# A decoder layer: an early expert tile from the first two batches, with its gate and up products and its transposes ahead of the index products

## Time and profile before

| | |
|---|---|
| median of three runs | 472.5 us (472.37 to 473.3) |
| the profiled execution | 473.93 us, of which 472.2 us are the span from its first to its last instruction |
| TensorE clock granted over the span | 0.955 of full |
| busy: PE, DVE, POOL, ACT | 420.8, 312.3, 221.1, 211.2 us |
| chain that ended last, by engine | PE 66%, DVE 17%, POOL 6%, issue 5%, DMA 3%, ACT 2% |
| batch 3 of the loop, to its last sum | about 250 to 309 us of the span |
| after the loop, to the first product of slot 1 | 309 to 345 us |
| slots 1 to 10 | 345 to 472 us, PE busy all through until 464 |

### The profile page before, as it was taken

The page is one execution under the profiler, slowest core; times in us unless marked ns, Lnnn a source line. Parts: engine busy times, 40 slices in busy tenths (PEclk is TensorE's granted clock), DMA queues, the critical chain, the costliest instruction groups (busy, mean ns, idle before and its releaser), DMA issues.

```text
span 472.2 us, 7846 instructions
## 1 busy us (share of the span) xinstructions
PE 420.8 (89%) x2560; PEld 212.2 (45%) x2561; DVE 312.3 (66%) x626; ACT 211.2 (45%) x412; POOL 221.1 (47%) x246
## 2 busy tenths in 40 slices
PE   4989588878998998989989899986999999999993
PEld 3444222333443443444434444354556666666652
DVE  3497778999987878878888786588214333334344
ACT  2456717564664557745577457612121111112220
POOL 2000615877986679967799578600551111111001
PEclk9998765798999999999999999999999999999997
DMA  9689940937365182756324430079120000000000
GB/s 237 91 279 108 301 144 12 146 119 115 89 138 110 68 134 70 134 180 199 137 78 169 159 112 0 1 287 361 55 55 11 12 4 9 11 11 11 11 1 9
DMA packets 39366, 49.36 MB, mean 105 GB/s; under 512 B 4664, under 2 KB 32673, under 8 KB 39334
## 3 DMA queue, kind: packets, MB, share of 16 engines
q1 hardware_dynamic: 36322, 46.65, 39.0%
q0 software_dynamic: 1056, 2.10, 1.5%
q10 hardware_dynamic: 1956, 0.21, 0.4%
HBM read 40.72 MB, written 8.91 MB: 105 GB/s over the span
## 4 chain that ended last, share of the span: by engine, by line
PE 66%; DVE 17%; POOL 6%; issue 5%; DMA 3%; ACT 2%; POOLq 0%; SPq 0%; DVEq 0%; ACTq 0%
PE ps L1181 16%; PE ps L1197 8%; PE ps L883 8%; PE ps L910 6%; PE ps L914 5%; PE ps L956 4%; PE ps L783 4%; DVE arena L1572 3%; DVE arena L1523 3%; DVE arena L1505 3%; PE ps L943 3%; PE ps L1189 2%; DMA arena<-arena 2%; POOL arena L655 2%; POOL arena L661 2%
## 5 line engine op out<-in xcount | busy, mean ns | idle before, releaser
L1372 ACT ACTIVATE arena<-ps 128x512 f32<-128x512 f32 x128 | 76.1, 595 | 84.9 <-PE ps L943 84.7
L1523 DVE TENSOR_REDUCE arena<-ps 128x2 f32<-128x512 f32 x128 | 86.6, 681 | 26.8 <-PE ps L914 22.7
L661 POOL TENSOR_TENSOR arena<-arena 128x512 f32<-128x512 f32 x60 | 76.8, 1279 | 36.2 <-DVE arena L1572 36.2
L655 POOL TENSOR_TENSOR arena<-arena 128x512 f32<-128x512 f32 x64 | 84.4, 1321 | 9.0 <-issue 8.8
L1181 PE MATMUL ps<-arena 128*128 x176 | 77.5, 593 | 0.7 <-ACT arena L1413 0.7
L1572 DVE TENSOR_TENSOR_SCAN arena<-ps,arena 128x512 f32<-128x512 f32 x60 | 72.8, 1214 | 0.5 <-DVE mv L1617 0.2
L883 PE MATMUL ps<-arena,identf 128*128 128x512 f32 x128 | 68.9, 625 | 0.0
L910 PE MATMUL ps<-arena 48*128 48x256 bf16 x256 | 52.7, 288 | 13.4 <-DVE arena L1523 10.0
L1331 ACT ACTIVATE ps<-arena 128x255 f32<-128x255 f32 x128 | 60.4, 473 | 1.9 <-DVEq L1726 1.9
L1839 DVE TENSOR_TENSOR arena<-arena,ps 128x1024 f32<-128x1024 f32 x11 | 13.4, 1222 | 59.9 <-ACT arena L1417 59.9
L731 POOL DMA_INDIRECT out<-rows_s,arena x11 | 10.8, 984 | 88.7 <-DVE rows_s L1868 80.5
(11 more groups left out here) (231 smaller groups left out, 524.7 us busy)
## 6 DMA issues: line engine op xcount, KB each, us to landing
arena<-bc_d SPq DMA_DIRECT2D x32, 512.0 KB, 4.4
arena<-in_L_ffn_Wg SPq DMA_DIRECT2D x8, 512.0 KB, 6.1
arena<-in_L_ffn_Wu SPq DMA_DIRECT2D x8, 512.0 KB, 5.9
arena<-in_L_ffn_Wd SPq DMA_DIRECT2D x4, 1024.0 KB, 11.7
arena<-kp_d SPq DMA_DIRECT2D x8, 384.0 KB, 7.9
arena<-qp_d SPq DMA_DIRECT2D x8, 384.0 KB, 10.8
qp_d<-arena SPq DMA_DIRECT2D x4, 384.0 KB, 8.5
kp_d<-arena SPq DMA_DIRECT2D x4, 384.0 KB, 8.4
```

The lines of the kernel that those rows point to most:

```text
L655: g.tensor_tensor(dBu[m % 3], dtu[:, :, b * SEQ:(b + 1) * SEQ], over_k(bcr[c % BC_RING][:, m % 2, 0, :]), ALU.mult).then_inc(dbu_ready, 1)
L661: g.tensor_tensor(h, h, over_k(bcr[m // 2 % BC_RING][:, m % 2, 1, :]), ALU.mult).then_inc(hc_ready, 1)
L1372: A(prob[2 * (slot % 2) + kt][:, pr * HALF:(pr + 1) * HALF], ps[:, 2 + n % 2, :], ACT.Exp).then_inc(p_ready, 1)
L1523: v.tensor_reduce(negm[b % 2][:, qt, 2 * pair:2 * pair + 2], ps[:, bank, :].rearrange("p (h k) -> p h k", h=2), axis=AX.X, op=ALU.max).the ...
```

## The change

**What is computed stays the same.** Slot 0 becomes an "early tile". Its 128 rows are the first 128 tokens of one expert among the first four token tiles (batches 0 and 1, 512 tokens in four experts, so at least one expert has 128). They are known once the logits of batch 1 are, in batch 3 of the loop. The remaining tokens fill slots 1 to 10 as before; there are still 11 slots.

- DVE gets five new groups inside batch 3: `early_experts` at (3, 2, 1), `early_counts` at (3, 3, 0), `early_choice` at (3, 4, 0), `early_ranks` at (3, 5, 0), `early_marks` at (3, 6, 0): 10, 3, 7, 7 and 4 instructions. PE gets `count_early` (two products, one more turn of the banks) at (3, 3, 0).
- POOL's `routing_constants` move from m = 56 to m = 49 and grow from ten fills to fourteen.
- PE picks the early rows (`pick_rows(EARLY, ...)`, 8 products) right after the loop, and ACT copies them (`take_x(0)`) ahead of its copy for the late logits.
- The gate and up product of slot 0 is cut into four halves. One stands ahead of `route_late(3)`, two ahead of the counting products, one behind them, in the places of 2, 10 and 10 of the fillers. Ahead of the first half PE waits for all gate and up weights and loads the expert's number.
- The picked rows of the old kind (8 tiles) now serve slot 1. `make_h(0)` on DVE stands behind the row masks, ahead of the index marks, and `turn_h(0)` on PE ahead of the index products. Slot 1 enters the loop without `gate_up(0)`, `turn_x(1)`, 8 fillers and `turn_h(0)` between the index products and it.
- POOL gathers slots 2, 0, 1 first; the first row handed to PE is slot 2.

On PE, behind the second transpose of the last batch (L1135; L1194 in the changed kernel) and up to the slots, there stood: fillers L871, the late logits L1111, the two counting products L1146 and L1147, the row picks L1154, the index products L1161.

The diff, cut to what matters:

```diff
@@ POOL: routing_constants, and where it is called
                 link(g.memset(resets, 1.0))
                 link(g.memset(resets[:, :, 0:1], 0.0))
+                link(g.memset(resets1, 1.0))
+                link(g.memset(resets1[:, :, 0:1], 0.0))
+                link(g.memset(placed[:, EXPERTS, :], 0.0))
+                link(g.memset(reached1[:, 0:1], 0.0))
...
-                if m == 3 * STATES + 8:
+                if m == 3 * STATES + 1:
                     routing_constants()
@@ PE: the loop, and after it
+            def count_early():
+                pe.wait_ge(early_oh, 1)
+                pe.wait_ge(consts, 4)
+                bank = turn()
...
+                        if b == BATCH - 1 and (qd, i) == (3, 0):
+                            count_early()
...
+            pe.wait_ge(y_out, BATCH)
+            pick_rows(EARLY, early_rows, early_ready)
             pe.wait_ge(x2_ready, 2 * (BATCH - 1))
             turn_late(BATCH - 2)
...
-            keep_warm(2, 5)
+            pe.wait_ge(wgu_in, 16 * 16)
+            pe.wait_ge(xcur_ready, 2)
+            first_expert = pe.value_load(estar_int[0:1, 0:1], min_val=0, max_val=EXPERTS - 1)
+            gate_up_half(0, first_expert)
             route_late(BATCH - 1)
-            keep_warm(10, 7)
+            for half in (1, 2):
+                gate_up_half(half, first_expert)
             pe.wait_ge(oh_ready, 1)
...
-            keep_warm(14, 4)
+            gate_up_half(3, first_expert).then_inc(gu_done, 1)
+            keep_warm(4, 4)
...
+            pick_rows(TT, first_rows, first_ready)
+            turn_h(0)
             pe.wait_ge(expert_ready, 1)
...
-            pe.wait_ge(wgu_in, 16 * 16)
-            gate_up(0, first_expert)
-            turn_x(1)
-            keep_warm(8, 6)
-            turn_h(0)
             pe.wait_ge(wd_in, 16 * 4)
             with pe.Fori(1, SLOTS - 1) as s:
@@ DVE: the new groups (each link() waits for its own instruction)
+            def first_of_max(tiles):
+                link(v.tensor_copy(run[:, tiles], oh[:, tiles, 0]))
+                v.tensor_copy(ohb[:, 0, tiles], oh[:, tiles, 0]).then_inc(logit_dve, 1)
+                for e in range(1, EXPERTS):
+                    link(v.tensor_tensor(ohb[:, e, tiles], oh[:, tiles, e], run[:, tiles], ALU.is_gt))
+                    link(v.tensor_tensor(run[:, tiles], run[:, tiles], oh[:, tiles, e], ALU.max))
+            def early_experts():
+                two = slice(0, EARLY)
+                link(v.tensor_reduce(lmax[:, two], lg[:, two, :], axis=AX.X, op=ALU.max))
+                link(v.tensor_tensor(oh[:, two, :], lg[:, two, :], lmax[:, two]..., ALU.is_ge))
+                first_of_max(two)
+                dve.sem_inc(early_oh, 1)
+            def early_counts():
+                bank = turn()
...
+                link(v.tensor_tensor_scan(out=incl1..., data0=resets1..., data1=ps[:, bank, n:2 * n], ...))
+                link(v.tensor_tensor(within1, incl1, earlier1, ALU.add))
+                link(v.tensor_tensor(within1, within1, total1, ALU.subtract))
+                dve.sem_inc(taken, 1)
+            def early_choice():
+                link(v.tensor_scalar(enough, incl1[:, :, EARLY - 1], float(P), None, ALU.is_ge))
+                link(v.tensor_tensor_scan(out=best, data0=ones32[:, 0:EXPERTS], data1=enough, ...))
...
+            def early_marks():
+                for t in range(EARLY):
+                    v.tensor_scalar(early_rows[t], lanes, float(P + 1), lane1[:, t:t + 1], ALU.add,
+                                    ALU.is_equal).then_inc(early_ready, 1)
...
+                        if b == BATCH - 1 and (qd, i) == (2, 1):
+                            dve.wait_ge(taken, turns.count)
+                            early_experts()
+                        if b == BATCH - 1 and (qd, i) == (3, 0):
+                            early_counts()
+                        if b == BATCH - 1 and (qd, i) == (4, 0):
+                            early_choice()
+                        if b == BATCH - 1 and (qd, i) == (5, 0):
+                            early_ranks()
+                        if b == BATCH - 1 and (qd, i) == (6, 0):
+                            early_marks()
@@ DVE: after the row masks of the slots
+            make_h(0)
...
+            link(v.tensor_tensor(e_of[:, 0:1], e_of[:, 0:1], estar, ALU.add))
```

More of the change, by code:

```diff
@@ L216, in decoder_layer @@
         run = carve(TT)
-        within = carve(EXPERTS * TT, EXPERTS, TT)
+        placed = carve((EXPERTS + 1) * TT, EXPERTS + 1, TT)
+        within, of_early = placed[:, 0:EXPERTS, :], placed[:, EXPERTS, 0:EARLY]
+        incl1 = carve(EXPERTS * EARLY, EXPERTS, EARLY)
+        within1 = carve(EXPERTS * EARLY, EXPERTS, EARLY)
+        resets1 = carve(EXPERTS * EARLY, EXPERTS, EARLY)
+        enough = carve(EXPERTS)
+        reached1 = carve(EXPERTS + 1)
+        best = carve(EXPERTS)
+        estar = carve(1)
+        estar_int = carve(1, dt=I32)
+        rank1 = carve(EARLY)
+        lane1 = carve(EARLY)
+        keep = carve(EARLY)
+        early_rows = [carve(P) for _ in range(EARLY)]
         incl = carve(EXPERTS * TT, EXPERTS, TT)
@@ L737, in _ @@
             pool.wait_ge(idx_ready, 1)
-            for s in (1, 0, 2):
+            for s in (2, 0, 1):
                 gather(s)
-            hand_row(1)
+            hand_row(2)
             for s in range(3, SLOTS):
@@ L1096, in expert_of, with gate_up_half, pick_rows, turn_h @@
                 return pe.value_load(e_int[0:1, bass.ds(s, 1)], min_val=0, max_val=EXPERTS - 1)
+            def gate_up_half(half, e):
+                w, fh = (wg_s, wu_s)[half // 2], half % 2
+                for k in range(KT):
+                    last = mm(ps[:, half, :], xcur[:, k, :], w[:, bass.ds((e * KT + k) * DFF + fh * HALF, HALF)],
+                              start=(k == 0), stop=(k == KT - 1))
+                return last
+            def pick_rows(tiles, marks, ready):
+                for t in range(tiles):
+                    pe.wait_ge(ready, t + 1)
+                    for k in range(KT):
+                        last = mm(ps[:, 7, k * P:(k + 1) * P], xres[:, t, k * P:(k + 1) * P], marks[t],
+                                  start=(t == 0 and k == 0), stop=(t == tiles - 1), skip_group_check=True)
+                last.then_inc(xt_pe, 1)
+            def turn_h(s):
+                pe.wait_ge(h_ready, s + 1)
+                for f in range(FT):
+                    last = nc.tensor.transpose(ps[:, 4 + f // 4, (f % 4) * P:(f % 4 + 1) * P],
+                                               hcur[:, f * P:(f + 1) * P], identf[:, :])
+                last.then_inc(ht_pe, 1)
             def turn_late(b):
@@ L1177, in gate_up @@
                 pe.wait_ge(xcur_ready, s + 2)
-                for w, b0 in ((wg_s, 0), (wu_s, 2)):
-                    for fh in range(2):
-                        for k in range(KT):
-                            last = mm(ps[:, b0 + fh, :], xcur[:, k, :],
-                                      w[:, bass.ds((e * KT + k) * DFF + fh * HALF, HALF)], start=(k == 0),
-                                      stop=(k == KT - 1))
-                last.then_inc(gu_done, 1)
-            def turn_h(s):
-                pe.wait_ge(h_ready, s + 1)
-                for f in range(FT):
-                    last = nc.tensor.transpose(ps[:, 4 + f // 4, (f % 4) * P:(f % 4 + 1) * P],
-                                               hcur[:, f * P:(f + 1) * P], identf[:, :])
-                last.then_inc(ht_pe, 1)
+                for half in range(4):
+                    last = gate_up_half(half, e)
+                last.then_inc(gu_done, 1)
             def down(s, e):
@@ new lines, in early_ranks @@
+            def early_ranks():
+                of_best = best.rearrange("p (e o) -> p e o", o=1).broadcast_to([P, EXPERTS, EARLY])
+                link(v.scalar_tensor_tensor(out=within1, in0=within1, scalar=1.0, in1=of_best, op0=ALU.add, op1=ALU.mult))
+                link(v.tensor_tensor(within1, within1, ohb[:, :, 0:EARLY], ALU.mult))
+                link(v.tensor_reduce(rank1, within1.rearrange("p e t -> p t e"), axis=AX.X, op=ALU.add))
+                link(v.scalar_tensor_tensor(out=lane1, in0=rank1, scalar=float(P), in1=rank1, op0=ALU.is_le, op1=ALU.mult))
+                link(v.tensor_scalar(of_early, lane1, -1.0, 0.0, ALU.add, ALU.max))
+                link(v.tensor_scalar(keep, lane1, 1.0, None, ALU.is_lt))
+                link(v.tensor_tensor(ohb[:, :, 0:EARLY], ohb[:, :, 0:EARLY],
+                                     keep.rearrange("p (o t) -> p o t", o=1).broadcast_to([P, EXPERTS, EARLY]), ALU.mult))
@@ L1777, in _ @@
             link(v.tensor_tensor(lg, lg, lmax3, ALU.subtract))
-            link(v.tensor_copy(run, oh[:, :, 0]))
-            v.tensor_copy(ohb[:, 0, :], oh[:, :, 0]).then_inc(logit_dve, 1)
-            for e in range(1, EXPERTS):
-                link(v.tensor_tensor(ohb[:, e, :], oh[:, :, e], run, ALU.is_gt))
```

(3 more changed lines are left out.)

70 lines of the change are left out of this document (43 added, 27 removed).

## The result

The changed kernel takes 477.24 us (median of 4 runs, 476.58 to 477.92), the kernel before 472.75 us in the same comparison: a ratio of 1.0094, 95% interval 1.0074 to 1.0114. It is slower by about 4.5 us. The forecast was 471.4 us and the range ended at 474.4 us.

The account below looks back on a forecast made before the run. PE bounds the slots, and batch 3, where PE, DVE and POOL have little room, and the tail count in full: 8.15 us cost less 9.2 us saved gives -1.05 us, so 472.5 becomes 471.4 us; range 466.8 to 474.4 us.

Parts of the forecast that it names:

- the second rival: Batch 3: TensorE's clock falls behind new waits; one fall costs 1.7 us (473.1 us), two give 474.8 us; chance 0.16.
- waits of 2.85 and 3.3 us: Batch 3: PE stands still behind `early_experts` (2.85 us) and `early_choice` (3.3 us), whose DVE instructions wait for POOL's.
- batch 3's waits: Batch 3: the new DVE groups and POOL's moved constants delay the loop by 0.1 + 2.85 + 1.4 + 3.3 + 0.5 = 8.15 us.
- the tail: Between loop and slots: slot 1's product starts at 335.9 instead of 345.07 us, 9.2 us saved (8.3 to 9.6).
- Rival 1: Batch 3: small DVE instructions slip between POOL's, so the groups cost 3.7 us; 467.0 us, chance 0.22.
- the three waits that it gave `early_choice`: Batch 3: three of its seven instructions wait for one POOL product each, until 283.4 us; the next copy moves 3.3 us.
- slot 1's product follows after some 0.15 us: Tail, on PE: gap between the index products' end at 335.76 us and slot 1's gate and up product.
- the register load: Tail, ahead of slot 0's first half: loading the expert's number on PE was taken as 0.3 us, between 0 and 1.
- 0.25 was booked: Tail: what is left of the early picks' push on the late logits, 0.25 us (0.1 to 0.4).
- Rival 3: Tail: returns only 8.3 us if the register load takes 1 us and late logits and counts hold DVE; 472.3 us, chance 0.08.
- The median: Whole kernel: the runs' median lies 1.4 us under the profiled execution, so the same -1.05 us was applied to 472.5 us.

Follow-up runs that it names:

- the constants split: The changed kernel with the early tile's seven routing constants between POOL's input and weighing of step 53, the rest at step 56 as before the change: 472.43 us, ratio 1.0007.
- the kinds run: The changed kernel with small four-column DVE instructions of several kinds, inputs in SBUF or PSUM, added in quads 0 and 1 of batch 3; its time is not compared.

## Why the prediction was wrong

**The step that failed** is the choice between the forecast and the second rival: "Against it: 2.3 us without any product around 324 left it at 1.00". That row, from another stretch, was taken to cover waits of 2.85 and 3.3 us, and the clock got 0.16 of the chance. The row also lies inside a wait. In the changed kernel the stretch inside the longer wait, from 284 to 288 us, was at 1.00 too, and the fall came behind it. Before the change the clock did stay at 1.00 behind that row (310 to 346 us), but the rows shown could not tell. In the changed kernel it fell behind the wait for `early_choice` and cost 2.55 us, where one fall had been priced at 1.7, and again at slot 1's product, 1.70 us, where no rival had a fall. Without these 4.25 us the profiled execution would have been 1.3 us ahead, 0.58 us of it from ahead of the change and 0.7 from the change itself; the forecast was 1.05. That these are near each other is partly luck: batch 3's waits were 0.8 us shorter than forecast, and the tail returned 1.1 us less.

How far this is shown: the wait of 3.53 us was followed by a fall in the profiled execution of the changed kernel and of five experiments that kept it, and by none where TensorE was busy in it or where it was shorter or gone (with `early_choice` a quad later, a new wait of 3.08 us came, and a fall behind that). The first wait, 2.6 to 2.7 us, was followed by a fall in four of the seven executions that kept it whole, and the wait for the second copy with the constants split, 2.30 us, by none. This last is in line with the earlier trace rows, so the row was right for a wait of its length and was stretched too far. In the four executions with a fall the first wait began between 265.6 and 266.7 us of the span, in the three without between 267.6 and 268.0; why that should matter is not shown. Slot 1's product took over 8.7 us in five of the seven executions that kept the two gaps ahead of it, and 7.0 to 7.2 us in all four with the gaps filled or gone; so the tail's fall goes with its gaps, but not each time.

**Batch 3's waits** were right one by one: 2.70, 1.42, 2.95 and 0.32 us against 2.95, 1.4, 3.3 and 0.5. That a DVE instruction waits for the end of POOL's is shown by the kinds run, and that POOL's order decides it, by the split constants. Rival 1 (no collisions for small instructions) is refuted by both. The prediction let the first instruction of `early_experts` pass without a reason; it is a reduction, and the kinds run shows that reductions pass. Of the three waits that it gave `early_choice`, the first took only 0.28 us (284.10, L1783), as it met the end of a product.

**The tail** returned 8.08 of 9.2 us. Two terms were too small. "slot 1's product follows after some 0.15 us": it followed after 0.90 us. With its expert's number loaded into a register ahead of the index products, and the loop's first pass written out in the same edit, the 0.90 us are gone; that the load and not the loop's entry was the larger part is argued from the first half, where the load alone was moved and 0.81 us went. And the first half began behind 0.65 us, where 0.3 was taken for the register load, and pushed the late logits: the marks (L1774 before) came 10.00 us late (333.07, L1888) where the loop's end was 9.36 us late, 0.64 us where 0.25 was booked. Rival 3 had named nearly this saving, 8.3 us, but for a load of 1 us ahead of the first half. That idle time was 0.65 us and gave 0.39 of the 1.1 us; the rest came from behind the index products, where no rival had anything. That its number came so near is luck.

**The median** was taken to move as the profiled execution does. It moved by 1.5 us more than the two profiled executions differ. 0.58 us of that lies in the part of the span that the change doesn't touch; for the rest the runs don't show why.

## What to carry to other kernels

A group of small instructions whose kinds wait for another engine's is priced by what that engine runs at that moment; with the same instructions and the same tail, moving the groups and POOL's constants decided between 4.5 us lost and 5.4 us gained. A wait that a change gives TensorE costs its own length and, beyond that, perhaps half speed behind it: price both, and take a row of a wait as long as the new one, in the same stretch, with the clock behind it, before the second is left out. If a group can't be moved, products that keep TensorE busy in its wait give back the second part but not the first. And before two profiled executions are set side by side, take their offset at a row that the change can't reach.

## What the runs showed that was not expected

- The load of a number from SBUF into a TensorE register, behind a wait, left TensorE idle for 0.81 us ahead of the first half; ahead of that wait it cost nothing.
- Fillers in a gap are not free once the gap is gone: with five of them slot 1's product began 0.66 us behind the index products, without them 0.03 us.
- Executions of one kernel differ in their mean clock. In the kernel with `early_choice` a quad later, runs went from 473.65 to 478.31 us, with mean clocks from 0.955 down to 0.942. Where the clock fell in those without a trace is not known.
